# Four-layer graph network on one core: grid points written before the second rows and fetched for one head at a time; layer 2's column factor moved into the exponential's bias

## Time and profile before

| what | value |
|---|---|
| runs | 1480.07, 1481.71, 1481.99 us; median 1481.71 |
| the profiled execution | 1480.52 us, its span 1478.8 us |
| TensorE (PE) busy | 1356.5 us, 92% of the span |
| VectorE (DVE) busy | 916.6 us, 62% |
| ScalarE (ACT) busy | 536.4 us, 36% |
| GpSimd (POOL) busy | 261.9 us, 18% |
| mean DMA rate | 217 GB/s |
| mean granted TensorE clock | 0.958 of full speed |

### The profile page before, as it was taken

The page is one execution under the profiler, slowest core; times in us unless marked ns, Lnnn a source line. Parts: engine busy times, 40 slices in busy tenths (PEclk is TensorE's granted clock), DMA queues, the critical chain, the costliest instruction groups (busy, mean ns, idle before and its releaser), DMA issues.

```text
span 1478.8 us, 11971 instructions
## 1 busy us (share of the span) xinstructions
PE 1356.5 (92%) x4222; PEld 682.6 (46%) x4222; DVE 916.6 (62%) x1333; ACT 536.4 (36%) x459; POOL 261.9 (18%) x235
## 2 busy tenths in 40 slices
PE   4887777899979999998999998999999999999994
PEld 2333334344444444454655454644445444544551
DVE  4787778888864000102115362599978987898565
ACT  4334334867630000000111100355554556455323
POOL 0000002880020000001000000133442224114211
PEclk9899997899989999999889999999999999999997
DMA  9999993000026766658447248688877888688201
GB/s 371 403 401 403 405 396 132 5 0 0 0 94 191 193 193 193 189 147 259 127 163 240 93 136 320 214 302 331 298 283 257 327 303 299 231 321 323 95 0 48
DMA packets 100470, 321.32 MB, mean 217 GB/s; under 512 B 11181, under 2 KB 26412, under 8 KB 86828
## 3 DMA queue, kind: packets, MB, share of 16 engines
q1 hardware_dynamic: 100395, 320.41, 61.9%
HBM read 316.94 MB, written 3.43 MB: 217 GB/s over the span
## 4 chain that ended last, share of the span: by engine, by line
PE 80%; DMA 9%; DVE 6%; ACT 3%; SPq 1%; issue 1%; POOL 0%; ACTq 0%; DVEq 0%
PE ps L1270 29%; PE ps L1083 10%; PE ps L1118 10%; PE ps L1023 9%; DMA ring<-in_adjB 7%; PE ps L1077 5%; PE ps L952 5%; PE ps L1180 2%; PE ps L1290 1%; DVE cols L1376 1%; PE ps L1252 1%; DMA y<-in_adj 1%; PE ps L1291 1%; PE ps L1099 1%; PE ps L1060 1%
## 5 line engine op out<-in xcount | busy, mean ns | idle before, releaser
L1270 PE MATMUL ps<-arena,x 128*128 128x512 f32 (+1 forms) x1092 | 438.9, 562 | 2.9 <-ACT shared L856 1.6
L1270 PEld LDWEIGHTS ps<-arena,x 128*128 128x128 f32 x1092 | 206.1, 190 | 231.3 <-issue 225.2
L849 ACT ACTIVATE arena<-arena,bench 128x3328 f32<-128x3328 bf16 x78 | 239.8, 3075 | 193.5 <-PE ps L1270 181.1
L952 PE MATMUL ps<-ring,bench 128*128 128x512 f32 (+1 forms) x364 | 173.1, 621 | 53.8 <-DMA ring<-in_adjB 53.8
L1906 DVE TENSOR_TENSOR arena<-arena,ring 128x3328 f32<-128x3328 f32 x51 | 184.7, 3621 | 26.9 <-ACT arena L849 26.9
L1083 PE MATMUL ps<-ring,x 128*128 128x512 f32 (+1 forms) x364 | 176.5, 567 | 0.0
L1118 PE MATMUL ps<-ring,x 128*128 128x512 f32 (+1 forms) x364 | 157.1, 587 | 9.2 <-DMA ring<-in_adjB 5.4
L630 POOL TENSOR_TENSOR ring<-ring,nid 128x128 f32<-128x128 f32 x51 | 98.7, 1935 | 199.4 <-DMA ring<-in_adjR 199.4
L952 PEld LDWEIGHTS ps<-ring,bench 128*128 128x128 f32 x364 | 71.7, 208 | 133.3 <-issue 123.7
L1627 DVE SCALAR_TENSOR_TENSOR bench<-b,cols,ps 128x128 f32<-128x128 f32 x26 | 7.3, 343 | 192.3 <-PE ps L1060 192.3
L1118 PEld LDWEIGHTS ps<-ring,x 128*128 128x128 f32 x364 | 71.5, 199 | 84.2 <-issue 69.9
(11 more groups left out here) (286 smaller groups left out, 1438.6 us busy)
## 6 DMA issues: line engine op xcount, KB each, us to landing
ring<-in_adjB SPq DMA_DIRECT2D x468, 256.0 KB, 3.7
ring<-in_adjR SPq DMA_DIRECT2D x51, 1664.0 KB, 8.3
arena<-in_adjR SPq DMA_DIRECT2D x27, 1664.0 KB, 8.2
shared<-in_adj SPq DMA_DIRECT2D x7, 1664.0 KB, 8.1
es<-in_adj SPq DMA_DIRECT2D x7, 1664.0 KB, 8.0
ring<-in_adjB SPq DMA_DIRECT2D x78, 128.0 KB, 2.5
xT<-in_adj SPq DMA_DIRECT2D x6, 1664.0 KB, 8.5
y<-in_adj SPq DMA_DIRECT2D x6, 1664.0 KB, 8.6
```

Of the source, the lines that this page charges most:

```text
L849: A_(E[n % 3], below[n % 3], ACT.Exp, bias=tt_[:, t * HEADS + k:t * HEADS + k + 1], scale=-WIN).then_inc(e_exp, 1)
L952: mm(ps[:, b, 0:w], lhsT=scaled[:, t % 4], rhs=ring[:, n % CHUNKS, 0:w], start=(t == 0), stop=(t == TILES - 1)).then_inc(ring_free, 1)
L1270: last = mm(ps[:, b, 0:w], lhsT=x[:, t], rhs=E[n % 3][:, o_:o_ + w], start=(t == 0), stop=(t == TILES - 1))
```

## The change

Three things change in the order of SP, and layer 2's column factor goes another way.

- SP writes the points at tile 6 of block 5 without waiting for the write, loads the two rows at tile 8 instead of tile 0, and at tile 18 waits for the write and fetches the table of head 0 alone. The tables of heads 1 and 2 are fetched in the heads' row loop, behind rows 6 and 10.
- Layer 2's sums use `x` itself as weights. The factor exp(-0.2 gap) is now a bias (`faint = -0.2 gap`) of the exponential, and `less_gap = -gap` takes the place of `back` in the tiles that ScalarE does alone. The denominator's column is made by putting ones in x's last column: GpSimd keeps that column aside, writes ones after the last transpose, and puts it back when the last sums are done.
- ScalarE computes one exponential of a single column ahead of the transposes' copies, with a result that nobody uses; with it comes the load of the exponential's table.

```diff
-        rs, sd, D, dg, mn, fin, back, rz = (cols[:, k, :] for k in range(8))
-        mean, var, diff, std, rstd, nf2, gap, fade = (cols[:, k, :] for k in range(8, 16))
+        rs, sd, D, dg, mn, fin, less_gap, rz = (cols[:, k, :] for k in range(8))
+        mean, var, diff, std, rstd, nf2, gap, faint = (cols[:, k, :] for k in range(8, 16))
+        aside = nf2
...
-        SPREAD_AT = 8
+        WRITE_AT, ROWS_AT, SPREAD_AT = 6, 8, 18
+        POINTS_AT = {6: 1, 10: 2}
...
+            def spread_points(k):
+                sp.dma_start(tops[k], points_kept[k:k + 1].to_broadcast([P, NP])).then_inc(points_in[k], 16)
+
             for n, b, t, o_, w in chunks():
...
-                if b == SUMS + 2 and t == 0:
+                if b == SUMS + 2 and t == WRITE_AT:
+                    sp.wait_ge(points_out, 1)
+                    sp.dma_start(points_kept.rearrange("k (t p) -> (k t) p", p=P), points).then_inc(points_written, 16)
+                if b == SUMS + 2 and t == ROWS_AT:
                     sp.wait_ge(sw_done, NB)
                     sp.dma_start(rows[0], d["adjR"][0]).then_inc(row_in[0], 16)
                     sp.dma_start(row_at(1), d["adjR"][1]).then_inc(row_in[1], 16)
                 if b == SUMS + 2 and t == SPREAD_AT:
-                    sp.wait_ge(points_out, 1)
-                    sp.dma_start(points_kept.rearrange("k (t p) -> (k t) p", p=P), points).then_inc(points_written, 16)
                     sp.wait_ge(points_written, 16)
-                    for k in range(HEADS):
-                        sp.dma_start(tops[k], points_kept[k:k + 1].to_broadcast([P, NP])).then_inc(points_in[k], 16)
+                    spread_points(0)
                 ring_load(R3, n, b, t, w)
...
                 for n in range(2, HEADS * TILES):
                     ge(sp, q_ready, n - 2)
                     sp.dma_start(rows[n % 3], d["adjR"][n % TILES]).then_inc(row_in[n % 3], 16)
+                    if n in POINTS_AT:
+                        spread_points(POINTS_AT[n])
...
-            pool.wait_ge(x_done, TILES)
-            pool.wait_ge(fade_done, 1)
-            g_.tensor_copy(y[:, :, F - 1:F], fade[:, :, None]).then_inc(xp_done, 1)
-            for t in range(TILES):
-                g_.tensor_scalar(y[:, t, 0:F - 1], x[:, t, 0:F - 1], fade[:, t:t + 1], None, ALU.mult).then_inc(xp_done, 1)
-
             def layer2(general):
                 if general:
                     return
+
+                pool.wait_ge(turned, NB)
+                g_.tensor_copy(aside[:, :, None], x[:, :, F - 1:F]).then_inc(aside_done, 1)
+                pool.wait_ge(aside_done, 1)
+                g_.memset(x[:, :, F - 1:F], 1.0).then_inc(aside_done, 1)
+                pool.wait_ge(sums1, NB)
+                g_.tensor_copy(x[:, :, F - 1:F], aside[:, :, None]).then_inc(aside_done, 1)
+                pool.wait_ge(aside_done, 3)
                 for k in range(GROUPS):
...
             for g in range(GROUPS - 3, GROUPS):
                 dot(g)
 
+            A_(zf[:, 0:1], ones[:, 0:1], ACT.Exp)
+
...
-                    A_(fade, gap, ACT.Exp, scale=-ALPHA).then_inc(fade_done, 1)
                     row_scores(0)
...
-                        A_(EL[t % 4], EL[t % 4], ACT.Exp, scale=1 - ALPHA, bias=back[:, t:t + 1]).then_inc(exp1, 1)
+                        A_(EL[t % 4], EL[t % 4], ACT.Exp, scale=1 - ALPHA, bias=less_gap[:, t:t + 1]).then_inc(exp1, 1)
...
-                        A_(EL[t % 4], EL[t % 4], ACT.Exp, scale=ALPHA - 1).then_inc(exp1, 1)
+                        A_(EL[t % 4], EL[t % 4], ACT.Exp, scale=ALPHA - 1, bias=faint[:, t:t + 1]).then_inc(exp1, 1)
...
                 for t in range(TILES):
-                    pe.wait_ge(xp_done, t + 2)
+                    if t == 0:
+                        pe.wait_ge(aside_done, 2)
...
-                        op = mm(ps[:, b, 0:w], lhsT=y[:, t], rhs=EL[t % 4][:, o_:o_ + w], start=(t == 0), stop=(t == TILES - 1))
+                        op = mm(ps[:, b, 0:w], lhsT=x[:, t], rhs=EL[t % 4][:, o_:o_ + w], start=(t == 0), stop=(t == TILES - 1))
...
-                    step(v.tensor_scalar(back, gap, ALPHA - 1, None, ALU.mult))
+                    v.tensor_scalar(faint, gap, -ALPHA, None, ALU.mult)
+                    step(v.tensor_scalar(less_gap, gap, -1.0, None, ALU.mult))
```

More of the change, by code:

```diff
@@ L221, in program @@
         q1_part = sem("q1_part")
-        fade_done = sem("fade_done")
-        xp_done = sem("xp_done")
+        aside_done = sem("aside_done")
         low1 = sem("low1")
@@ L512, in heads @@
                     sp.wait_ge(win_done, NB)
-                    for k in range(HEADS):
-                        sp.wait_ge(points_in[k], 16)
+                    sp.wait_ge(points_in[0], 16)
                     sp.wait_ge(gru_done, GROUPS)
@@ L730, in layer2 @@
                             act.wait_ge(low1_part, n + 1)
-                            A_(EL[0][:, lo:hi], EL[0][:, lo:hi], ACT.Exp, scale=ALPHA - 1).then_inc(exp1_part, 1)
+                            A_(EL[0][:, lo:hi], EL[0][:, lo:hi], ACT.Exp, scale=ALPHA - 1, bias=faint[:, 0:1]).then_inc(exp1_part, 1)
                     else:
                         act.wait_ge(low1, MIN_TILES.index(t))
-                        A_(EL[t % 4], EL[t % 4], ACT.Exp, scale=ALPHA - 1).then_inc(exp1, 1)
+                        A_(EL[t % 4], EL[t % 4], ACT.Exp, scale=ALPHA - 1, bias=faint[:, t:t + 1]).then_inc(exp1, 1)
                 def relu_pair(k):
@@ L823, in heads @@
                     act.wait_ge(row_in[1], 16)
-                    for k in range(HEADS):
-                        act.wait_ge(points_in[k], 16)
                     for k in range(HEADS):
@@ L989, in layer2 @@
                     mm(ps[:, 7, 0:P], lhsT=ones[:], rhs=hb[:, 0], start=True, stop=True).then_inc(gl_row, 1)
-                    pe.wait_ge(xp_done, TILES + 1)
                     pe.wait_ge(rp_done, RP_ACT)
```

## The result

The changed kernel takes 1471.35 us (median of four, 1470.98 to 1471.6) against 1481.85 for the kernel before on the same chip: a ratio of 0.9932, 95% interval 0.9915 to 0.9949. That is 10.5 us less where I had forecast 7.5, inside the range of 1471.2 to 1478.0, though at its lower end. The profiled execution took 1471.27 us, its span 1469.5 against 1478.8: 9.3 us less in this pair of profiles.

A forecast was written before the change was run, and what follows sets the result against it. TensorE carries the span, so only its idle columns or lower-clock time can be gained. -7.11 + 0.1 + 0 - 0.4 - 0.1 = -7.5 us gave a median of 1474.2 us, range 1471.2 to 1478.0.

The forecast's parts named there:

- The stop: Layer 4's first product (L1118), before 909.11 us: TensorE idle 4.63 us plus 2.48 us at the slower clock, 7.11 together.
- (a): SP in block 5: write of the points at tile 6, wait for it at tile 18; -7.11 us.
- (b): Two row loads moved from tile 0 to tile 8 of block 5: 0.78 us gap reappears as 0.9, counted +0.1.
- (c): Only head 0's table fetched in the ring, heads 1 and 2's in the heads: hidden, counted 0.
- D: Delay of the heads' row 7 behind table 1: taken as 2.4 to 4.2 us, free up to 5.2 us.
- (d): Layer 2: table load and fade exponential leave ScalarE's path, which starts up to 1.0 us earlier; counted -0.4 us.
- (f): DVE's cuts (L1572) without GpSimd's scaling beside them: 0.08 us each for a few, counted -0.1 us.
- the copy back: Layer 2's end: GpSimd puts x's last column back while ScalarE takes the sums out; counted as nothing.
- layer 2 gives more: Rival, 9%: layer 2's whole 1.0 us, block 5's 0.8 us gap gone, shorter DVE operations; 1471.7 us.
- the tables stop the heads: Rival, 4%: the heads' rows 7 and 11 late behind tables 1 and 2; 1485.0 us at the longest landing, 8.1.
- P: Experiments' theory for 3.2 us between L1077 and L1180: where low-clock stretches fall relative to the work decides, whatever was edited.

The follow-up runs named there:

- after_late: The changed kernel with one 128x1024 copy on ScalarE ahead of the root that ends layer 2, delaying layer 3 by 2.3 us: 1474.89 us, ratio 0.9962.
- after_plus1: The changed kernel with one extra 128x1024 square root on ScalarE ahead of the one that ends layer 2: 1473.16 us, ratio 0.9949.
- rows_apart: The changed kernel with the first of the two rows loaded at tile 0 of block 5, the other at tile 8: 1471.78 us, ratio 0.9933.
- the table alone: The kernel before with one added exponential of a column ahead of the transposes' copies: 1481.1 us, ratio 0.9997.
- layer2_only: The changed kernel with SP's old order, so only layer 2's edits and the early table load: 1477.79 us, ratio 0.997.
- rows_at_0: The changed kernel with both rows back at tile 0 of block 5, ahead of the write of the points: 1471.77 us, ratio 0.993.
- before_again: The kernel before, word for word, profiled again in one execution: 1483.72 us.
- sp_only: The kernel before with only SP's order changed, layer 2 as before: 1472.8 us, ratio 0.994.
- before_plus1: The kernel before with one extra 128x1024 square root on ScalarE ahead of the one that ends layer 2: 1482.48 us, ratio 1.0005.
- before_plus2: The kernel before with two extra 128x1024 square roots on ScalarE ahead of the one that ends layer 2: 1482.74 us, ratio 1.0005.

## Why the prediction was right, and where it was off

**The stop, (a) and (b): right.** The mechanism was as told: write out of the chain, no low clock behind it, tile 8 late instead. Forecast -7.11 + 0.1 = -7.0. Measured 117.7 against 123.7, -6.0, in the first pair. Over the seven profiles with the old order and the seven with a new one, the means are 123.3 and 116.4, -6.9. In the seven old ones the stop is 4.1 to 4.8 us long, and the fourteen records behind it take 7.7 to 9.3 us; none of the seven new ones has a stop, or lower clock there. Tile 8's gap, put at 0.9 us, was 1.85 here, 0.9 and 1.2 in two others, and 0 in three (`after_late`, `after_plus1`, `rows_apart`). The cover was as forecast: the rows went out at 886.86, tile 8 was wanted at 902.07 - 1.85 = 900.22, 13.4 us later. That the load had queued behind the two rows rests on its 14.21 us from issue to landing; why the gap is 1.85 us in one profile and 0 in another with the same order stays open.

**The tables in the heads, (c): right.** Row 7 of the heads, against the earlier trace rows:

```profile
973.39 1.31 POOL L637 TENSOR_TENSOR ring<-ring,nid 128x128 f32<-128x128 f32 x1 [5.39 <-DMA ring<-in_adjR]
...
975.50 3.61 DVE L1913 TENSOR_TENSOR arena<-arena,ring 128x3328 f32<-128x3328 f32 x1
```

With the 9.25 us by which everything is earlier, the row would have landed at 971.81; it came at 973.39, so D was 1.6 us (forecast 2.4), and the weighing starts at 984.75 - 9.25 = 975.50, to the hundredth. At row 11 DVE waited 0.42 us for GpSimd's cut, and TensorE never noticed: its idle time in the heads is still 2.9 us. The head's own table took no one's time either. What the prediction had wrong here is the gauge: the three tables landed 10.5 to 11.3 us after their issue, longer than the 8.1 us that it feared, and still D was 1.6. The delay was nearer to what the rate gave (2.4 us) than to any time to landing.

**Layer 2, (d) to (f): one term missing.** I had -0.4 and -0.1. The first sum came 0.2 us earlier, counted from L973 (19.4 against 19.6 us; 0.5 with the table alone); over all profiles it is 18.9 to 19.5 us with layer 2's edits and 19.6 to 19.7 in the six without them and without the early table, 0.5 us in the means, as forecast. The term that I had at nothing, the copy back "while ScalarE takes the sums out", goes with 0.4 us lost at GpSimd's first add. The copy itself was long done (425.86), so it is not its duration; what holds the add for half a microsecond the profile does not say. Layer 2 came out at +0.2 us in the first pair; the kernel before alone gave 185.0 and 185.8 us in its two profiles, so +0.2 cannot be told from the forecast.

**DVE beside GpSimd.** Without GpSimd's scaling, the longest cut goes from 2.05 to 1.95 us and the shorter of the two multiplications of tile 0 from 1.57 to 1.48; the other operations ahead of the first sum keep their durations within 0.02 us. So 0.1 us for all was about the right size. The Trainium skill (SBUF — State Buffer, "Who interferes with whom") says that whoever issues first keeps the shared pair of ports for the whole instruction, and that the order of issue decides who blocks. So the rule does not say that VectorE loses, as I had taken it to. The trace of before fits it with VectorE first: VectorE's cuts lost at most 0.1 us each, and GpSimd's 26 scalings took from 0.6 to 7.3 us each.

**What the sum lacked, and luck.** The forecast had no term for time at the lower clock other than that behind the stop. It should have had one with both signs: the stretch from L1077 to L1180 is worth 381.2 to 385.7 us, by how much of it falls to the lower clock. In the first pair it gave -3.2. The pair adds up as -0.3 + 0.2 - 3.2 - 6.0 = -9.3 us; the medians differ by 10.5, because the profiled execution of the kernel before was 1.3 us faster than its median. So the time fell inside the range, 0.15 us from its lower end, with 3 us in it that no term of the forecast stood for: the mechanism of the stop was right, and that the sum stayed in the range was in part luck. A second thing is outside any edit: L973, at the end of layer 1, starts at 255.8 us in the mean of the seven kernels with layer 2's edits and at 257.1 in the other seven, before an edited instruction of SP, DVE or TensorE has run. The two profiles of the kernel before differ there by 1.4 us among themselves (256.0 and 257.4). Why layer 1 differs stays open; it was not tried.

**Of the rivals,** "layer 2 gives more" had forecast 1471.7, close to the measured time and for the wrong reason: DVE gave nothing more, and the gap of (b) grew. The rival that the tables stop the heads had its break-even at D = 6.5; D was 1.6.

**How far P is settled.** Shown: the 3.2 us are time at the lower clock (the sum over the fourteen profiles above). Shown, each by the single profile of a run: layer 2's edits do not by themselves bring them (`after_plus1`, `rows_apart`: all the edits, none of the gain), and with a delay alone they go (`after_late`). It is not the start of the work that decides, counted from the first instruction: L1077 starts at 440.9 us in the changed kernel, in `layer2_only` and in `after_plus1`, and only the first two are short; L973 starts at 256.0 in both `rows_at_0` and the kernel before. The low stretches themselves lie elsewhere: the one at the end of layer 3 begins 234.8 to 235.0 us after L1077's start in the four short profiles, 237.1 in the kernel before, 238.0 in `rows_apart` as in `before_again`. Not shown: what sets that place, and how often an untraced execution of the same kernel falls the other way. Each of the two kernels repeated its own in a second profile, but the executions of `rows_apart` (1469.74 to 1473.47 us) and `sp_only` (1472.3 to 1475.74) spread by as much as is in question.

No version was found that beats the changed kernel beyond the measurement's uncertainty: `rows_apart` removes the last wait for the ring, and its median is the same.

## What to carry to other kernels

A queue that issues the loads of the main stream must not wait for a round trip through DRAM: write, go on issuing, and wait for the write about as many loads later as the ring is deep (here twelve, with thirteen slots). Most of the gain is in that, 6 to 7 us here, and what the transfers' order does beside it is second. Value a stop as the idle time plus the slower clock behind it. Changes of a few microseconds move the work against TensorE's low-clock stretches, worth 3 to 4 us of either sign here, and that shows in busy time and not in any wait. So compare first starts of the same lines stage by stage, take half of the time at the lower clock out of the length of each stage that TensorE fills, and repeat with a harmless delay, and in more than one profile, before an edit is given credit.

## What the runs showed that I had not expected

- The same 52 small matmuls take 6.9 or 9.1 to 9.8 us, by the granted clock they meet. Both kernels repeated theirs in a second profile (6.9 and 6.9, 9.4 and 9.1); more executions were not traced.
- 1.0 and 2.0 us of work added in series on the path (`before_plus1`, `before_plus2`) changed the median by 1.2 and 1.5 us. The intervals of the ratios hold 1.0 as well as the full delay, so such a run alone can't tell 2 us from nothing.
- A table load hidden in a wait became visible (1.28 us) as soon as another function was put ahead of it on ScalarE.
- The issue of the points' write took SP 0.44 us at its new place against 0.93 at the old one.
